# Reciprocals of a fused attention and gated-cell kernel: through DRAM instead of PE transposes

## Chip, cores and metric

One core of one Trainium2 chip. The metric is the device time of one execution of the program in microseconds; the median of several executions counts.

## The reference

`x` and `ctx` are (8, 512, 512) in float32. First a cross attention with a local window, then a gated recurrence over the batch axis:

```python
q = layernorm(x); k = v = ctx                      # 16 heads of 32
scores = einsum(q, k) / sqrt(32); scores[|i - j| > 64] = -inf
x = x + softmax(scores) @ v @ W_proj.T + b_proj
z = layernorm(x)
for t in range(8):                                 # c is (512, 512)
    f = sigmoid(z[t] @ wf.T + c @ uf.T + bf)
    i = sigmoid(z[t] @ wi.T + c @ ui.T + bi)
    g = tanh(z[t] @ wc.T + c @ uc.T + bc)
    c = f * c + i * g
out = x + tanh(z @ wo.T + c @ uo.T + bo)
```

## The kernel before

The attention works on 32 tiles of 128 query rows (4 for each of 8 batch entries). A tile has four slots, one for each group of 4 heads. The recurrence of batch entry b is 12 units (3 gates by 4 groups of 128 outputs); a unit is a sum of 8 cell products (4 for entry 0, whose state is the same for all rows), each with a high and a low part of both operands, so that one product is three PE matmuls (L499 to L501, 128x512).

One list, `steps`, sets the order of all engines: each engine walks it in order and takes its own part of each step, with semaphores between them. The list is written by the loop at L133: for slot n, i = n // 4 is the tile and s = n % 4 the slot in the tile. From slot 20 on (`early` is false) a slot holds, in this order:

- `turn` n: PE transposes the exponentials of the slot (L542), ACT copies them to `probs_t` (L682)
- for s = 1 `query` of tile i + 1 (PE, L510), for s = 2 `turn2` of tile i - 1 (PE L607, ACT L702, DVE L822), for s = 3 `spread` of tile i (PE L586, ACT L686)
- two cell products
- `score` n + 2: PE (L523), then DVE adds the mask and takes the row minimum (L767); `ln2b` for s = 1 (L816), `mult` for s = 3 (L796)
- `exp` n + 1: ACT (L677); `value` n: PE (L563, L568)
- gates and blends whose cell products are complete (ACT L719; DVE L851 to L868), states of the entry (ACT L731, DVE L879)
- `recip` n + 1: DVE (L774), POOL (L483); `sides` n + 1: three or six small DVE transposes of `probs` (L790)
- for s = 0: `ln1b` of tile i + 1 (DVE L758), `proj`, `resid` and `stat2` of tile i - 1 (PE products L499 to L501 into `ps_m`, DVE L801), loads; for s = 3 `halves` of tile i (ACT L690, POOL L478)
- the remaining cell products: one for entry 0 (slots 20 to 34), four afterwards.

The sums of the exponentials lie one query per partition, but the attention, `ps_v`, has queries along its free axis and the head's dimensions along the partitions. So `recip` takes the reciprocal of the sums (`invsum`), POOL copies each over 32 columns (`recip`), four PE transposes turn the tile's 128x512 block into `ps_m` (`spread`), ACT copies that to `tile_row`, and DVE multiplies `ps_v` with it (`mult`):

```python
if kind == "spread":
    pe.wait_ge(inv, G * (i + 1))
    ...
    for g in range(G):
        mm = pe.transpose(ps_m[:, g * P:(g + 1) * P], recip[:, g, :], ident[:, :])
```

`value` of a tile's first slot overwrites `ps_v` and waits for that multiplication (`attn_t`, L550). `halves` splits the result into `attn_hi` and `attn_lo`, for which `proj` waits (L597). SP issues all loads and stores of the steps in list order, one after the other.

## Time and profile before

| | us |
|---|---|
| median of 3 runs (1013.83 to 1017.21) | 1015.32 |
| profiled execution | 1014.71 |
| its span | 1012.7 |
| PE busy in the span | 981.4 (97%) |
| DVE, ACT, POOL busy | 609.7, 500.7, 226.1 |
| chain that ended last | PE 90%, DVE 4%, ACT 2% |

A row of a timeline gives the start in us from the span's start, the length in us, engine and line of the kernel, the operation with output and inputs, the count where like instructions were merged, and in brackets the idle time before it and who released it. Ends of PE matmuls are modelled and overlap the next start, so distances between starts tell what one costs. The span has three parts: tiles 0 to 4 without cell products, to about 105 us; tiles 5 to 31 with cell products, to about 839 us; the output products.

### The profile page before, as it was taken

The page shows a single profiled execution, that of the slowest core. Times are in us where ns is not written, and L with a number is a line of the kernel's source. Part 1 is how long each engine was busy: PE and PEld are TensorE (multiplying, and loading weights), DVE is VectorE, ACT ScalarE, POOL GpSimd, SP SyncE. Part 2 cuts the span into 40 slices and gives each one's busy share as a digit, 9 for nine tenths or more (in the row PEclk, how much of TensorE's full clock was granted, in tenths as well). Part 3 has the DMA queues.
Part 4 walks back from the last instruction along what each step waited for, and adds up shares of the span by engine and source line. Part 5 has one row for each costly group of instructions (what it writes and reads, how often), then busy time and mean ns, then how long its engine had stood idle before and what let it go on. Part 6 is the DMA issues. An engine that isn't in the chain of part 4 may idle for free.

```text
span 1012.7 us, 20229 instructions
## 1 busy us (share of the span) xinstructions
PE 981.4 (97%) x7028; PEld 739.8 (73%) x7028; DVE 609.7 (60%) x2211; ACT 500.7 (49%) x1473; POOL 226.1 (22%) x320
## 2 busy tenths in 40 slices
PE   6888999999999999999999999999999999999998
PEld 3454566777777777777777777777777778888886
DVE  5775887776567755866677656765577632133222
ACT  5776666555454554554465455554455432131222
POOL 4554322211111111211111112111111110002354
PEclk9998999999999999999999999999999999999999
DMA  8455322222222212212222222111112003029676
GB/s 270 122 164 166 110 74 80 84 80 73 79 85 79 66 61 75 63 54 74 79 85 79 74 79 84 58 53 47 43 35 72 12 20 126 1 81 376 226 231 208
DMA packets 76245, 99.36 MB, mean 98 GB/s; under 512 B 5233, under 2 KB 46193, under 8 KB 74609
## 3 DMA queue, kind: packets, MB, share of 16 engines
q1 hardware_dynamic: 75424, 97.80, 30.6%
q8 instruction: 57, 0.93, 0.4%
q10 hardware_dynamic: 720, 0.27, 0.2%
q14 instruction: 44, 0.35, 0.1%
HBM read 68.69 MB, written 29.36 MB: 97 GB/s over the span
## 4 chain that ended last, share of the span: by engine, by line
PE 90%; DVE 4%; ACT 2%; issue 2%; DMA 1%; POOL 0%; SPq 0%; DVEq 0%; ACTq 0%
PE ps_g L499 18%; PE ps_g L501 17%; PE ps_g L500 17%; PE ps_a L523 7%; PE ps_a L542 4%; PE ps_v L563 3%; PE ps_m L499 3%; PE ps_m L501 3%; PE ps_m L500 3%; PE ps_m L594 2%; PE ps_a L499 2%; PE ps_a L500 2%; PE ps_a L501 2%; PE ps_v L568 2%; ACT probs L677 1%
## 5 line engine op out<-in xcount | busy, mean ns | idle before, releaser
L767 DVE CUSTOM_DVE_ANT_0 probs<-ps_a,mask 128x192 f32<-128x192 f32 (+1 forms) x512 | 169.3, 387 | 162.8 <-PE ps_a L523 153.3
L677 ACT ACTIVATE probs<-probs,rowmin 128x192 f32<-128x192 f32 (+1 forms) x512 | 239.1, 473 | 1.7 <-DVE rowmin L767 1.7
L719 ACT ACTIVATE gate<-ps_g,bias 128x512 f32<-128x512 f32 x84 | 57.8, 688 | 211.2 <-PE ps_g L501 211.2
L790 DVE STREAM_TRANSPOSE probs_t<-probs 32x128 f32<-32x128 f32 x492 | 146.5, 298 | 6.0
L483 POOL COPY recip<-invsum 128x128 f32<-128x128 f32 x128 | 37.4, 292 | 493.4 <-DVE invsum L774 493.2
L499 PE MATMUL ps_g<-state_hi,gate_w 128*128 128x512 f32 x336 | 138.2, 411 | 0.0
L682 ACT ACTIVATE probs_t<-ps_a 128x512 f32<-128x512 f32 x108 | 64.3, 596 | 147.1 <-PE ps_a L542 146.5
L501 PE MATMUL ps_g<-state_hi,gate_w 128*128 128x512 f32 x336 | 131.4, 391 | 0.0
L500 PE MATMUL ps_g<-state_lo,gate_w 128*128 128x512 f32 x336 | 131.3, 391 | 0.0
L677 ACT ACTIVATION_READ_ACCUMULATOR probs<-probs,rowmin 128x1 f32 x512 | 98.5, 192 | 0.0
L523 PE MATMUL ps_a<-keys,queries 32*128 32x256 f32 (+1 forms) x1024 | 86.1, 406 | 2.2 <-DVE rowmin L767 1.4
L499 PE MATMUL ps_g<-x2t_even,gate_w 128*128 128x512 f32 x192 | 82.2, 428 | 0.0
L499 PE MATMUL ps_g<-x2t_odd,gate_w 128*128 128x512 f32 x192 | 79.2, 412 | 0.0
L501 PE MATMUL ps_g<-x2t_even,gate_w 128*128 128x512 f32 x192 | 75.5, 393 | 0.0
L501 PE MATMUL ps_g<-x2t_odd,gate_w 128*128 128x512 f32 x192 | 75.3, 392 | 0.0
L500 PE MATMUL ps_g<-x2t_even,gate_w 128*128 128x512 f32 x192 | 75.2, 392 | 0.0
L500 PE MATMUL ps_g<-x2t_odd,gate_w 128*128 128x512 f32 x192 | 75.1, 391 | 0.0
L499 PEld LDWEIGHTS ps_g<-state_hi,gate_w 128*128 128x128 f32 x336 | 63.1, 188 | 14.7 <-issue 2.4
L523 PEld LDWEIGHTS ps_a<-keys,queries 32*128 32x128 f32 x1024 | 40.8, 186 | 45.1 <-issue 42.1
L501 PEld LDWEIGHTS ps_g<-state_hi,gate_w 128*128 128x128 f32 x336 | 63.1, 188 | 13.7
L500 PEld LDWEIGHTS ps_g<-state_lo,gate_w 128*128 128x128 f32 x336 | 63.3, 188 | 10.7
L542 PE MATMUL ps_a<-ident,probs 128*128 128x128 f32 x432 | 65.6, 272 | 0.4 <-ACT probs L677 0.2
(182 smaller groups left out, 1754.4 us busy)
## 6 DMA issues: line engine op xcount, KB each, us to landing
values<-ctx_rows SPq DMA_DIRECT2D x34, 256.0 KB, 4.4
xr<-x SPq DMA_DIRECT2D x32, 256.0 KB, 3.8
keys<-ctx_t SPq DMA_DIRECT2D x16, 512.0 KB, 4.1
x_dram<-xr SPq DMA_DIRECT2D x32, 256.0 KB, 4.2
gate_w<-x2t_dram SPq DMA_DIRECT2D x8, 1024.0 KB, 10.6
keys<-ctx_t SPq DMA_DIRECT2D x16, 384.0 KB, 3.5
x2t_dram<-x2t_even SPq DMA_DIRECT2D x12, 512.0 KB, 3.8
x2t_dram<-x2t_odd SPq DMA_DIRECT2D x12, 512.0 KB, 3.8
```

The costliest lines, as they stand in the source:

```text
L483: pool.tensor_copy(recip[:, i % G, :].rearrange("p (h d) -> p h d", h=HPG), invsum[:, i // G % 2, i % G, :].unsqueeze(2).to_broadcast([P, ...
L499: pe.matmul(ps, lhs[0], rhs[0], start=start, stop=False)
L500: pe.matmul(ps, lhs[0], rhs[1], start=False, stop=False)
L501: return pe.matmul(ps, lhs[1], rhs[0], start=False, stop=stop)
L523: mm = pe.matmul(ps_a[h][:, 0:seen], queries[rows, g, :], keys[rows, tile % 2, g, 0:seen], start=True, stop=True)
L542: mm = pe.transpose(ps_turn[i][:, h * P:(h + 1) * P], probs[:, i % 2, h, own:own + P], ident[:, :])
L563: pe.matmul(ps_v[HEAD * h:HEAD * (h + 1), g * P:(g + 1) * P], values[:, tile % 2, 0, d], probs_t[:, h, :], start=True, stop=False)
L677: act.activation(row, row, ACT.Exp, bias=rowmin[:, i % 2, h:h + 1], scale=-1.0, accum_out=rowsum[:, i // G % 2, i % G, h:h + 1]).then_inc( ...
L682: act.activation(probs_t[:, 0:HPG, :], ps_turn[i][:, :].rearrange("p (a q) -> p a q", a=HPG), ACT.Copy)\
L719: act.activation(gate[:, min(gt, 1), :], ps_g[i % 2][:, :], ACT.Tanh, bias=(first_bias if b == 0 else bias)[:, gt, m:m + 1], scale=1.0 if ...
L767: dve.tensor_tensor_reduce(probs[:, i % 2, h, 0:SEEN[t]], ps_a[h][:, 0:SEEN[t]], mask[:, MASK0[t]:MASK0[t] + SEEN[t]], -SCALE, -NEG, ALU.a ...
L790: turn = dve.transpose(probs_t[BLK * keys_of:BLK * (keys_of + 1), HPG:2 * HPG, q], probs[q, i % 2, :, col:col + BLK])
```

## The change

From tile 5 on, the spread on PE and ACT and the broadcast on POOL are gone. Instead the reciprocals of a tile are kept in 32 columns of `invsum` (16 in use), DVE transposes these in 32x32 blocks to `invsum_t`, SP writes this to `recip_dram`, waits for its landing, and reads it back with each row of 128 queries repeated over 32 partitions (`send`, once after the third slot's reciprocal for three groups, once after the fourth's for the last). `mult` and `halves` of a tile move to the head of the next tile, behind `turn`; `mult` reads the reciprocals from `recip`. In s = 0, part of the remaining cell products goes ahead of `proj`: two from slot 36 on, none before. `proj` also waits for `x2_lo`, since `spread` no longer does so in front of it. The small statistics tiles are joined in one, `moments`.

```diff
...
@@ -140,20 +140,21 @@
             tile_steps("stat2", i - 1)
         if n < SLOTS:
             steps.append(("turn", n))
+        if s == 0 and i > WHOLE:
+            tile_steps("mult", i - 1)
+            tile_steps("halves", i - 1)
         if n - 1 in row_at:
             steps.append(("column", row_at[n - 1]))
         if early:
             steps.append(("exp", n + 1))
         else:
             if s > 0:
-                tile_steps((None, "query", "turn2", "spread")[s], (None, i + 1, i - 1, i)[s])
+                tile_steps((None, "query", "turn2", None)[s], (None, i + 1, i - 1, -1)[s])
             cells(2)
         if n + 2 < SLOTS:
             steps.append(("score", n + 2))
         if s == 1:
             tile_steps("ln2b", i - 1)
-        if s == 3 and not early:
-            tile_steps("mult", i)
         if early:
             tile_steps(("proj", "query", "turn2", "spread")[s], (i - 1, i + 1, i - 1, i)[s])
         elif n + 1 < SLOTS:
@@ -167,12 +168,15 @@
         gates()
         if n + 1 < SLOTS:
             steps.append(("recip", n + 1))
+            if n + 1 >= OWN_BANKS and (n + 1) % G >= G - 2:
+                steps.append(("send", 2 * ((n + 1) // G) + (n + 1) % G - (G - 2)))
             if n + 1 >= OWN_BANKS:
                 steps.append(("sides", n + 1))
         if s == 0:
             tile_steps("ln1b", i + 1)
             tile_steps("bias", i + 1)
             if not early:
+                cells(PER_SLOT[min((n - FIRST_CELL) // (TT * G), B - 1)] // 2 - 1)
                 tile_steps("proj", i - 1)
                 tile_steps("resid", i - 1)
                 tile_steps("stat2", i - 1)
@@ -183,8 +187,6 @@
             tile_steps("ln1", i + 2)
         if s == 3 and early:
             tile_steps("mult", i)
-        if s == 3 and i >= WHOLE:
-            tile_steps("halves", i)
         if FIRST_CELL <= n < FIRST_CELL + 2:
             steps.append(("split_proj", PAIR * (n - FIRST_CELL)))
         if n in split_slots:
@@ -193,7 +195,8 @@
             steps.append(("half_bias", 0))
             steps.append(("halve_c0", 0))
         if n >= FIRST_CELL:
-            cells(PER_SLOT[min((n - FIRST_CELL) // (TT * G), B - 1)] - 2)
+            more = PER_SLOT[min((n - FIRST_CELL) // (TT * G), B - 1)] - 2
+            cells(more - more // 2 if s == 0 else more)
         renew()
         n += 1
         if n == SLOTS + G:
@@ -250,6 +253,7 @@
 
         probs_t = sb("probs_t", [P, 2 * HPG, P], F32)
         recip = sb("recip", [P, G, P], F32)
+        recip_row = recip[:, :, :].rearrange("p g q -> p (g q)")
         attn_hi = sb("attn_hi", [P, G, P], F32R)
         attn_lo = sb("attn_lo", [P, G, P], F32R)
 
@@ -261,19 +265,22 @@
         bp_row = sb("bp_row", [P, D], F32)
         rowmin = sb("rowmin", [P, 2, HPG], F32)
         rowsum = sb("rowsum", [P, 2, G, HPG], F32)
-        invsum = sb("invsum", [P, 2, G, HPG], F32)
+        invsum = sb("invsum", [P, HEAD], F32)
+        inv_rows = invsum[:, 0:HPG * G].rearrange("p (h g) -> p h g", h=HPG)
+        invsum_t = sb("invsum_t", [P, HEAD], F32)
...
@@ -387,6 +395,19 @@
                 if kind == "ln2b":
                     sp.wait_ge(x1_done, i + 1)
                     sp.dma_start(x1_rows[i], xr[:, i % XR, :]).then_inc(x1_out[i % XR], DMA)
+                if kind == "send":
+                    tile, part = i // 2, i % 2
+                    sent = i - 2 * WHOLE
+                    sp.wait_ge(inv_turned, sent + 1)
+                    sp.dma_start(recip_dram[i].rearrange("c (a j) -> a c j", j=HEAD), invsum_t[:, :])\
+                      .then_inc(recip_sent, DMA)
+                    sp.wait_ge(recip_sent, DMA * (sent + 1))
+                    sp.wait_ge(spread, WHOLE)
+                    sp.wait_ge(attn_t, tile)
+                    first, last = (0, (G - 1) * P) if part == 0 else ((G - 1) * P, G * P)
+                    rows = recip_dram[i, 0:HPG * G, :].rearrange("(h g) q -> h (g q)", h=HPG)[:, first:last]
+                    sp.dma_start(recip_row[:, first:last],
+                                 rows.unsqueeze(1).to_broadcast([HPG, HEAD, last - first])).then_inc(recip_in, DMA)
                 if kind == "turn2" and b < B - 2:
                     sp.wait_ge(x2_lo, i + 1)
                     sp.dma_start(x2t_dram[b, :, :, :, t * P:(t + 1) * P],
@@ -477,11 +498,11 @@
                     need(pool, projected, i)
                     pool.tensor_tensor(attn_lo[:, :, :], attn, attn_hi[:, :, :].bitcast(F32), ALU.subtract)\
                         .then_inc(attn_split, 1)
-                if kind == "recip":
+                if kind == "recip" and i < OWN_BANKS:
                     pool.wait_ge(inverted, i + 1)
                     need(pool, spread, i // G)
                     pool.tensor_copy(recip[:, i % G, :].rearrange("p (h d) -> p h d", h=HPG),
-                                     invsum[:, i // G % 2, i % G, :].unsqueeze(2).to_broadcast([P, HPG, HEAD]))\
+                                     inv_rows[:, :, i % G].unsqueeze(2).to_broadcast([P, HPG, HEAD]))\
                         .then_inc(inv, 1)
                 if kind == "stat2":
                     pool.wait_ge(var2, i + 1)
@@ -586,6 +607,7 @@
                         mm = pe.transpose(ps_m[:, g * P:(g + 1) * P], recip[:, g, :], ident[:, :])
                     mm.then_inc(spread, 1)
                 if kind == "proj":
+                    need(pe, x2_lo, i)
                     if i == 0:
                         pe.wait_ge(wp_in, DMA)
                     if i < WHOLE:
@@ -736,6 +758,7 @@
 
         @block.vector
         def _(dve):
+            dve.memset(invsum[:, :], 0.0).then_inc(padded, 1)
             dve.wait_ge(consts, 6)
             for kind, i in steps:
                 if kind == "ln1":
@@ -770,8 +793,16 @@
                 if kind == "recip":
                     r, g = i // G % 2, i % G
                     dve.wait_ge(expd, HPG * (i + 1))
-                    need(dve, inv, i - 2 * G + 1)
-                    dve.reciprocal(invsum[:, r, g, :], rowsum[:, r, g, :]).then_inc(inverted, 1)
+                    if i == 0:
+                        dve.wait_ge(padded, 1)
+                    need(dve, inv, min(i - G + 1, OWN_BANKS))
+                    need(dve, inv_turned, 2 * (i // G - WHOLE) + (g == G - 1))
+                    dve.reciprocal(inv_rows[:, :, g], rowsum[:, r, g, :]).then_inc(inverted, 1)
+                if kind == "send":
+                    sent = i - 2 * WHOLE
+                    dve.wait_ge(inverted, G * (i // 2) + G - 1 + i % 2)
+                    need(dve, recip_sent, DMA * sent)
+                    dve.transpose(invsum_t[:, :], invsum[:, :]).then_inc(inv_turned, 1)
                 if kind == "turn" and i < OWN_BANKS:
                     some = min(SEEN[i // G % TT] - P, P)
                     dve.wait_ge(turned_2, i + 1)
@@ -791,9 +822,15 @@
                                              probs[q, i % 2, :, col:col + BLK])
                     turn.then_inc(turned_b, 1)
                 if kind == "mult":
-                    dve.wait_ge(recip_out, i + 1)
                     dve.wait_ge(valued, G * (i + 1))
-                    dve.tensor_tensor(tile_row[:, :], ps_v[:, :], tile_row[:, :], ALU.mult).then_inc(attn_t, 1)
+                    if i < WHOLE:
+                        dve.wait_ge(recip_out, i + 1)
+                        dve.tensor_tensor(tile_row[:, :], ps_v[:, :], tile_row[:, :], ALU.mult).then_inc(attn_t, 1)
+                    else:
+                        dve.wait_ge(recip_in, 2 * DMA * (i - WHOLE + 1))
+                        dve.wait_ge(q_turned, min(i + 2, TILES))
+                        dve.wait_ge(x2_turned, i)
+                        dve.tensor_tensor(tile_row[:, :], ps_v[:, :], recip_row, ALU.mult).then_inc(attn_t, 1)
                 if kind == "resid":
                     row = xr[:, i % XR, :]
                     dve.wait_ge(projected, i + 1)
...
```

PE from the end of the score product in the first slot of tile 17. Before:

```order
L523 MATMUL ps_a<-keys,queries 128x256 x3
L563 MATMUL ps_v<-probs_t,values 32x128 [waits v_in1,attn_t,turned_b,turned_a]
L563 MATMUL ps_v<-probs_t,values 32x128 x3
L568 MATMUL ps_v<-probs_t,values 32x128 x4
L499 MATMUL ps_m<-proj_w,attn_hi 128x512 [waits attn_split,wp_lo]
L500 MATMUL ps_m<-proj_w,attn_hi 128x512
L501 MATMUL ps_m<-proj_w,attn_lo 128x512
L499 MATMUL ps_m<-proj_w,attn_hi 128x512
L500 MATMUL ps_m<-proj_w,attn_hi 128x512
L501 MATMUL ps_m<-proj_w,attn_lo 128x512
```

After:

```order
L544 MATMUL ps_a<-keys,queries 128x256 x3
L584 MATMUL ps_v<-probs_t,values 32x128 [waits v_in1,attn_t,turned_b,turned_a]
L584 MATMUL ps_v<-probs_t,values 32x128 x3
L589 MATMUL ps_v<-probs_t,values 32x128 x4
L520 MATMUL ps_g<-x2t_odd,gate_w 128x512
L521 MATMUL ps_g<-x2t_odd,gate_w 128x512
L522 MATMUL ps_g<-x2t_odd,gate_w 128x512
L520 MATMUL ps_g<-x2t_odd,gate_w 128x512
L521 MATMUL ps_g<-x2t_odd,gate_w 128x512
L522 MATMUL ps_g<-x2t_odd,gate_w 128x512
L520 MATMUL ps_m<-proj_w,attn_hi 128x512 [waits attn_split,wp_lo,x2_lo]
L521 MATMUL ps_m<-proj_w,attn_hi 128x512
```

The three rows of a cell product stand twice between the value products (L563 and L568, now L584 and L589) and the projection, which was next to them before.

DVE from the last mask of the fourth slot of tile 16 to the first mask of the next slot. Before:

```order
L767 ISA probs,rowmin<-ps_a,mask 128x256
L767 ISA rowmin 128x1
L796 TENSOR_TENSOR tile_row<-ps_v,tile_row 128x512 [waits valued,recip_out]
L865 SCALAR_TENSOR_TENSOR gate<-gate,state 128x512 [waits gated]
L868 SCALAR_TENSOR_TENSOR state<-gate 128x512 [waits kept]
L774 RECIPROCAL invsum<-rowsum 128x4 [waits inv,expd]
L790 STREAM_TRANSPOSE probs_t<-probs 32x4x32 [waits valued,expd]
L790 STREAM_TRANSPOSE probs_t<-probs 32x4x32 x5
L767 ISA probs,rowmin<-ps_a,mask 128x256 [waits turned_b,expd,scored]
```

After:

```order
L790 ISA probs,rowmin<-ps_a,mask 128x256
L790 ISA rowmin 128x1
L902 SCALAR_TENSOR_TENSOR gate<-gate,state 128x512 [waits gated]
L905 SCALAR_TENSOR_TENSOR state<-gate 128x512 [waits kept]
L800 RECIPROCAL invsum<-rowsum 128x4 [waits inv_turned,inv,expd]
L821 STREAM_TRANSPOSE probs_t<-probs 32x4x32 [waits valued,expd]
L821 STREAM_TRANSPOSE probs_t<-probs 32x4x32 x5
L833 TENSOR_TENSOR tile_row<-ps_v,recip 128x512 [waits q_turned,x2_turned,recip_in,valued]
L790 ISA probs,rowmin<-ps_a,mask 128x256 [waits turned_b,expd,scored]
```

The multiplication stood ahead of blends, reciprocal and side blocks, and now stands behind them, ahead of the next masks.

SP from the store of `x1` in the second slot of a tile on. Before:

```order
L389 DMA x_dram<-xr 128x512 [waits x1_done]
L392 DMA x2t_dram<-x2t_odd 1024x1x128 [waits x2_lo]
L362 DMA xr<-x 128x512 [waits x2_done,x1_out3]
L365 DMA keys<-ctx_t 128x4x192 [waits scored]
```

After:

```order
L397 DMA x_dram<-xr 128x512 [waits x1_done]
L402 DMA recip_dram<-invsum_t 4x32x32 [waits inv_turned]
L409 DMA recip<-recip_dram 128x1x384 [waits attn_t,spread,recip_sent]
L413 DMA x2t_dram<-x2t_odd 1024x1x128 [waits x2_lo]
L402 DMA recip_dram<-invsum_t 4x32x32 [waits inv_turned]
L409 DMA recip<-recip_dram 128x1x128 [waits attn_t,spread,recip_sent]
L370 DMA xr<-x 128x512 [waits x2_done,x1_out3]
L373 DMA keys<-ctx_t 128x4x192 [waits scored]
```

Two pairs of a write and a read of `recip_dram` are new, one ahead of the store of `x2t` and one behind it, and with them a wait of SP for each write.

## Rows read from the trace of the kernel before

**Rows 1.** Busy us by stretch: length, PE, PEld, DVE, ACT, POOL; PEclk; DMA share, GB/s.
```profile
195.00:802.00 607.00, 607.00 (x4577) 463.76 (x4576) 405.35 (x1528) 318.16 (x967) 107.07 (x176) 1.00 0.22 66
```

**Rows 2.** PE: one tile's line, then the timeline (start us, us, engine, line).
```profile
L586 PE MATMUL ps_m<-ident,recip x128: 272/273/329, 24.1 to 822.6; 128*128 128x128 f32 x128
...
408.95 0.60 PE L542 MATMUL ps_a<-ident,probs 128*128 128x128 f32 x4
...
409.74 0.48 PE L499 MATMUL ps_g<-x2t_even,gate_w 128*128 128x512 f32 x1
...
415.26 0.60 PE L542 MATMUL ps_a<-ident,probs 128*128 128x128 f32 x4
415.62 0.48 PE L499 MATMUL ps_g<-x2t_odd,gate_w 128*128 128x512 f32 x1
```

**Rows 3.** Timeline of PE, turns with `recip` set in the early slots.
```profile
122.96 0.60 PE L542 MATMUL ps_a<-ident,probs 128*128 128x128 f32 x4
124.30 0.66 PE L586 MATMUL ps_m<-ident,recip 128*128 128x128 f32 x4 [0.73 <-POOL recip L483]
124.71 0.48 PE L499 MATMUL ps_g<-x2t_even,gate_w 128*128 128x512 f32 x1
...
187.34 0.60 PE L542 MATMUL ps_a<-ident,probs 128*128 128x128 f32 x4
...
189.19 0.48 PE L499 MATMUL ps_g<-x2t_even,gate_w 128*128 128x512 f32 x1
```

**Rows 4.** Timeline of DVE around the heads at 415.26 and 443.26.
```profile
413.45 0.69 DVE L796 TENSOR_TENSOR tile_row<-ps_v,tile_row 128x512 f32<-128x512 f32 x1
...
415.47 1.85 DVE L790 STREAM_TRANSPOSE probs_t<-probs 32x128 f32<-32x128 f32 x6
...
435.52 0.17 DVE L774 RECIPROCAL invsum<-rowsum 128x4 f32<-128x4 f32 x1
```

**Rows 5.** Timeline of PE from the head at 415.26.
```profile
417.83 0.43 PE L563 MATMUL ps_v<-probs_t,values 128*32 128x128 f32 x8
...
418.40 0.50 PE L499 MATMUL ps_m<-proj_w,attn_hi 128*128 128x512 f32 x1
...
424.42 0.60 PE L510 MATMUL ps_m<-ident,tile_row 128*128 128x128 f32 x4
...
443.26 0.60 PE L542 MATMUL ps_a<-ident,probs 128*128 128x128 f32 x4
```

**Rows 6.** Timelines of ACT and POOL around the same head.
```profile
414.17 0.63 ACT L690 ACTIVATE attn_hi<-tile_row 128x512 fp32r<-128x512 f32 x1
...
416.39 0.50 ACT L677 ACTIVATE probs<-probs,rowmin 128x256 f32<-128x256 f32 x1
...
415.87 1.30 POOL L478 TENSOR_TENSOR attn_lo<-tile_row,attn_hi 128x512 fp32r<-128x512 f32 x1
```

**Rows 7.** Timelines of PE and DVE around two early heads.
```profile
128.30 0.63 PE L542 MATMUL ps_a<-ident,probs 128*128 128x128 f32 x3
...
137.53 0.63 PE L510 MATMUL ps_m<-ident,tile_row 128*128 128x128 f32 x4 [0.61 <-DVE xr L801]
...
151.09 1.01 PE L542 MATMUL ps_a<-ident,probs 128*128 128x128 f32 x4
...
158.56 0.60 PE L510 MATMUL ps_m<-ident,tile_row 128*128 128x128 f32 x4
...
130.25 1.85 DVE L790 STREAM_TRANSPOSE probs_t<-probs 32x128 f32<-32x128 f32 x6
...
146.61 0.17 DVE L774 RECIPROCAL invsum<-rowsum 128x4 f32<-128x4 f32 x1
```

**Rows 8.** DMA issues (out<-in, queue, count, KB each, us from issue to landing).
```profile
values<-ctx_rows SPq DMA_DIRECT2D x44, 128.0 KB, 4.2
...
out<-xr SPq DMA_DIRECT2D x20, 256.0 KB, 2.1
...
values<-x_dram SPq DMA_DIRECT2D x8, 256.0 KB, 6.3
```

More of the change, by code:

```diff
@@ L21, in bass_xattn_ffn @@
 def bass_xattn_ffn(nc, x, ctx_rows, ctx_t, w_proj, b_proj, w_gates, u_gates, biases, w_out, u_out, b_out, in_c,
-                   out, x1_dram, x2t_dram):
+                   out, x1_dram, x2t_dram, recip_dram):
     B, T, D = x.shape
@@ L269, in bass_xattn_ffn @@
         st1 = sb("st1", [P, 2, 6], F32)
-        mv1 = sb("mv1", [P, 2, 2], F32)
-        ve1 = sb("ve1", [P, 2], F32)
-        rs1 = sb("rs1", [P, 2], F32)
         st2 = sb("st2", [P, 2, 6], F32)
-        mv2 = sb("mv2", [P, 2, 2], F32)
-        ve2 = sb("ve2", [P, 2], F32)
-        rs2 = sb("rs2", [P, 2], F32)
+        moments = sb("moments", [P, 4, 4], F32)
+        mv1, mv2 = [moments[:, a, :].rearrange("p (r m) -> p r m", r=2) for a in range(2)]
+        ve1, rs1 = moments[:, 2, 0:2], moments[:, 2, 2:4]
+        ve2, rs2 = moments[:, 3, 0:2], moments[:, 3, 2:4]
         ps_a = [pb(f"ps_a{h}") for h in range(HPG)]
@@ L290, in bass_xattn_ffn @@
         x2t_out = [sem("x2t_out0"), sem("x2t_out1")]
+        recip_sent = sem("recip_sent"); recip_in = sem("recip_in")
         raw_in = sem("raw_in"); bo_in = sem("bo_in")
@@ L300, in bass_xattn_ffn @@
         stat1 = sem("stat1"); aggr1 = sem("aggr1"); var1 = sem("var1"); ln1 = sem("ln1")
-        masked = sem("masked"); inverted = sem("inverted"); turned_b = sem("turned_b"); cleared = sem("cleared")
+        masked = sem("masked"); inverted = sem("inverted"); inv_turned = sem("inv_turned"); padded = sem("padded"); turned_b = sem("turned_b"); cleared = sem("cleared")
         attn_t = sem("attn_t"); x1_done = sem("x1_done")
@@ L932 @@
     B, T, D = arrays["x"].shape
+    recip_dram = nc.dram_tensor("recip_dram", (2 * B * T // P, HEAD, P), F32, kind="Internal").ap()
     x2t_dram = nc.dram_tensor("x2t_dram", (B, P, 2, D // P, T), F32, kind="Internal").ap()
@@ L935 @@
                    [d["w_c"], d["w_i"], d["w_f"]], [d["u_c"], d["u_i"], d["u_f"]],
-                   [d["b_c"], d["b_i"], d["b_f"]], d["w_out"], d["u_out"], d["b_out"], d["in_c"], out, x1_dram, x2t_dram)
+                   [d["b_c"], d["b_i"], d["b_f"]], d["w_out"], d["u_out"], d["b_out"], d["in_c"], out, x1_dram, x2t_dram,
+                   recip_dram)
     r = run_bass_kernel_spmd(nc, [arrays], core_ids=[0])
```

## Prediction

> **What bounds the kernel now.** I read the busy time by stretch first, then the idle time of PE in front of its instructions, then the timeline of each engine around one head of a tile, then the DMA issues. From 195 to 802 us PE is busy for 607.00 of 607.00 us at a granted clock of 1.00, while DVE has 405 and ACT 318 [rows 1]: in this stretch the span is the sum of PE's instructions, and an instruction taken from PE is a gain unless a new wait fills the hole. Before it, from 105.42 to 194.73, lie the sixteen slots of batch 0's cell (three cell products a slot), where other engines set part of the pace. I call them the early slots, those after them the steady ones.
>
> **What the change removes from PE.** The four transposes of `recip` per tile, from tile 5 on: 27 sets. Each lasts 273 ns by itself, but they overlap, so I take the distance between starts. With the set, the first transpose of the turn starts at 408.95 and the next cell product at 409.74: 0.79 us. Without it, 415.26 to 415.62: 0.36 us, elsewhere 0.35 [rows 2]. A steady set costs 0.44 us, and there are 23: **10.1 us**. In the early slots there are four sets, and there PE also waits for POOL's broadcast of the reciprocals (0.73 us at 124.30). The same distances are 1.75 us in the first (122.96 to 124.71) and 1.85 in the last (187.34 to 189.19) [rows 3], with 1.48 and 1.59 between them; less 0.35 each this is **5.3 us**. ACT's copy of `ps_m` to `tile_row` and POOL's 108 broadcasts go too; both engines have idle time, so I cost them at nothing. Moving two cell products ahead of the projection costs PE nothing by itself.
>
> **What it moves: the head of a tile.** The multiplication now stands at the head of the next tile, and PE needs it at that slot's value product. Take the head at 415.26, with the heaviest load on DVE (six side blocks, two blends). Before, DVE does the multiplication at 413.45 (0.69 us, its tail overlapped) and the side blocks from 415.47 to 417.32 [rows 4]. Without the multiplication in front, they end at about head + 1.4, the multiplication at + 2.1; the value product starts at + 2.57 (417.83) [rows 5]. So it is in time by 0.5 us. ACT's rounding (0.63) and POOL's subtraction (1.30) [rows 6] then end at + 2.7 and + 4.1; the projection, before at + 3.14 (418.40) [rows 5], is wanted two products (1.37 us) later, at + 4.5. Hidden by 0.4 us: no cost. What is late next is ACT's exponentials of that slot: they start after the rounding, at + 2.7 where they stood at + 1.1 (416.39) [rows 6], and end at + 4.7, still before DVE is through with its masks and asks for them. Only where a state is rounded behind them does DVE's chain (state, reciprocal, side blocks, next normalization, residual) pass the query's transposes, at + 9.15: by about 0.1 us at the first steady head and at five later ones. I charge **0.5 us**.
>
> In the early slots no cell product stands ahead of the projection, and every head has a state to round. At 128.30 the side blocks end at + 3.8 [rows 7]; after the change at + 3.2, the multiplication at + 3.9, the rounding at + 4.6, the subtraction at + 5.9. PE wanted the projection at + 4.5. The exponentials end at + 6.7, state at + 8.0, side blocks at + 10.0, normalization and residual at + 11.3, and the query's transposes wait for that: before they start at + 9.23 (137.53) [rows 7]. That is **2.1 us** given back. At 151.09 only three side blocks stand in front; the same walk puts the subtraction at + 4.7, the end of the projection at + 7.6, the query at + 8.9, against + 7.47 (158.56) before: **1.4 us**, and again 1.4 at the third head.
>
> **What it adds.** Two DVE transposes of 128x32 per tile (no row of this size; the side block is 0.31 us, nothing is the other end; 0.1 to 0.3 each, I take 0.1 because each partition has a quarter of the side block's elements). They stand in the second and third slots of a tile, where DVE idles: nothing. On SP's queue come four DMAs per tile, and SP waits in between for its own write to land; queued behind it are the store of `x2t`, the next `load_x` and `load_k`. Those buffers are used most of a tile (some 27 us) later: nothing. What matters is the chain from the last reciprocal to the multiplication: write of 16 KB, then broadcast read of 64 KB. The rows bound a transfer: 2.1 us for a store of 256 KB, 4.2 for loads of 128 KB [rows 8]. Between 4.2 and 8.4 us for the pair I take 2.1 for the write, since it is a store, and the middle, 3.2, for the read, plus 0.3 for transpose and hand-over: 5.6 us. In the steady slots the reciprocal ends at 435.7 and the next head is at 443.26, or 442.8 without the set; the multiplication may start at head + 1.9: 9.0 us are there [rows 4, 5]. Hidden, even at 8.4. In the early slots there are 6.3 us at the first head, 5.2 at the second (146.78 to 149.96 + 2.0) [rows 7] and about 5.1 at the third: late by 0.4 and 0.5, **0.9 us**.
>
> The Trainium skill, "DMA: Bandwidth & Descriptors" (the section on the two cost components), states a fixed 2.0 us and 436 GB/s. By it the pair would take an estimated 4.2 us and the 0.9 us would go. No row here shows so small a store.
>
> **Sum.** 10.1 + 5.3 - 0.5 - 2.1 - 1.4 - 1.4 - 0.9 = 9.1 us. The profiled execution took 1014.7 (span 1012.7), so 1005.6 like for like; against the median of 1015.3 it gives **1006.2 us**. Terms after the attention (PE's output products) just shift.
>
> **Rivals.**
> (a) *The early waits do not come back.* PE's 5.3 us there stay gone, because the delayed engines catch up during the projection. For: PE's wait for DVE's residual in front of the query was only 0.61 us [rows 7]. Against: in each head multiplication, rounding, exponentials and state lie in one chain. Time: 1015.3 - 15.4 = 1000.
> (b) *The early transfers are late by the upper bound.* With 8.4 + 0.3 us for the pair the three heads lose 2.4, 3.5 and 3.6 us in place of 0.9: 1015, no change.
> (c) *The wait only changes its name at every head.* The steady margins are 0.4 and 0.5 us. If the multiplication or POOL's part is 0.9 us longer than walked, each of 24 heads gives back what its set saved: 1015 to 1016. Against: rows 4 to 6 measure every part.
> (d) *Slower: the round trip through memory paces each tile.* The point is 9.0 us; from 9.4 on a head loses more than its 0.44. The loads with 6.3 us [rows 8] give 12.6 + 0.3 for the pair: 3.9 us at 24 heads, some 7.5 at three: about 1120 us. DVE would stand at the multiplication, behind it its masks, on PE the value product. Against: 6.3 us belongs to a burst of loads at the end; the middle moves 66 GB/s [rows 1].
> (e) *Each transpose is worth its full length.* 108 x 273 ns = 29.5 us: 986. Against: a set takes 0.44 us of PE's time, and PE overlaps [rows 2]. The Trainium skill, "TensorE: Matmul & The Clock Gate", Part 4 (PE-mode transpose), gives about 275 ns for a 128x128 transpose within a kernel, which the 273 ns agree with; by it alone an estimated 29.7 us would go.
> (f) The change does what it says as far as PE's list shows: 27 sets are gone from it.
>
> **Chances.** Forecast with its own spread (1003 to 1010) 0.55; (a) 0.20; (b) 0.11; (c) 0.06; (d) 0.05; (e) 0.03. The range runs from (a) to 1011: it leaves out (c), (d), (e) and half of (b). About 0.3% (3 us) is what a measurement here can tell from no change, so faster means below 1012.3: all of the forecast, (a), (e) and half of (b), 0.84. Same is the rest of (b) and most of (c), 0.10; slower 0.06.
>
> **What would show it.** Right: `recip` transposes on PE fall from 128 to 20; a turn takes 0.35 us to the next cell product in the fourth slot; PE stays at 607 of 607 in the steady stretch; idle time appears before the projection and the query at three early heads, 1 to 2 us each; the pair of transfers takes 5 to 6 us. Wrong: idle time at the value product of steady heads, released by DVE's multiplication or a DMA, (c) or (d); no idle time at early heads, (a); early heads waiting for a DMA by 2 us and more, (b).

## The result, and the profile after

| | before | after |
|---|---|---|
| median, us | 1014.58 (1013.38 to 1017.21) | 1025.3 (1022.47 to 1029.49) |
| profiled execution | 1014.71 | 1026.02 |
| its span | 1012.7 | 1024.2 |
| PE, DVE busy | 981.4, 609.7 | 979.4, 625.0 |
| ACT, POOL busy | 500.7, 226.1 | 487.2, 194.9 |

The ratio of the times is 1.0109, with a 95% interval of 1.009 to 1.0127: **slower by 1.1%**, where the forecast was 1006.2 with a range of 1000 to 1011.

Page of the changed kernel: span, engines, granted clock in 40 slices, chain that ended last.

```profile
span 1024.2 us, 20049 instructions
...
PE 979.4 (96%) x6920; PEld 734.9 (72%) x6920; DVE 625.0 (61%) x2266; ACT 487.2 (48%) x1446; POOL 194.9 (19%) x212
...
PEclk9999988889999999999999999999999999999999
...
PE 85%; DVE 5%; DMA 4%; issue 2%; ACT 2%; SPq 1%; POOL 1%; DVEq 0%; ACTq 0%
```

PE has 108 instructions fewer, yet its busy time fell by 2.0 us only, and the clock shows why one should look early: four slices of 25.6 us, from 128 to 230, are at 8 tenths. The same line of the kernel before:

```profile
PEclk9998999999999999999999999999999999999999
```

It has 9 there. DMA, 1% of the chain before, is 4%.

To see where the time goes I took the start of each slot's `turn` on PE and subtracted the same slot's start before, both counted from the turn of slot 20. A growing number is time lost, and each part of the kernel answers for its own growth. Each of these numbers comes from one profiled execution; times and ratios are of medians. Up to slot 38 (the early slots and the fourth head) the changed kernel loses **20.6 us** (229.05 - 103.98 = 125.07, before 209.88 - 105.42 = 104.46). From there to slot 127 it gains **7.15 us**. From a head's turn to the next slot's it loses 4.7, 6.8, 8.2 and 5.5 us at the four early heads; in the slots without the set it gains 0.8, 0.7, 1.2 and 1.0, and 0.8 once more in the slot behind the first head. All that is lost is lost at four places. The four sets are worth 3.8 us there; the 0.8 behind the first head is not theirs, since experiment 10 keeps the sets and shows it too.

The steady stretch, busy time as in [rows 1]; then PE's waits from 104 to 215 us (total, times, longest).

```profile
195.00:802.00 607.00, 603.20 (x4514) 456.34 (x4513) 421.23 (x1583) 309.80 (x955) 82.93 (x89) 0.99 0.27 80
```

```profile
PE ps_v L584 <- DVE tile_row L833: 12.6, 4, 4.5
...
PE ps_m L520 <- POOL attn_lo L499: 3.5, 3, 1.5
```

In the steady stretch PE is busy for 603.2 of 607 us, and part of the missing 3.8 is the fourth head at 208. In the early slots it waits four times for the multiplication, for 12.6 us. The third early head, on each engine. PE first:

```profile
178.13 1.12 PE L563 MATMUL ps_a<-ident,probs 128*128 128x128 f32 x4
...
185.68 0.66 PE L584 MATMUL ps_v<-probs_t,values 128*32 128x128 f32 x8 [4.50 <-DVE tile_row L833]
...
187.70 0.76 PE L520 MATMUL ps_m<-proj_w,attn_hi 128*128 128x512 f32 x1 [1.14 <-POOL attn_lo L499]
...
190.82 0.63 PE L521 MATMUL ps_m<-proj_w,attn_hi 128*128 128x512 f32 x1
191.25 0.63 PE L522 MATMUL ps_m<-proj_w,attn_lo 128*128 128x512 f32 x1
...
192.98 0.40 PE L521 MATMUL ps_g<-x2t_even,gate_w 128*128 128x512 f32 x1
193.21 0.39 PE L522 MATMUL ps_g<-x2t_even,gate_w 128*128 128x512 f32 x1
```

DVE and SP at the same place:

```profile
175.21 0.21 DVE L805 STREAM_TRANSPOSE invsum_t<-invsum 128x32 f32<-128x32 f32 x1
...
184.85 0.69 DVE L833 TENSOR_TENSOR tile_row<-ps_v,recip 128x512 f32<-128x512 f32 x1 [4.10 <-issue]
...
175.54 0.56 SPq L413 DMA_DIRECT2D x2t_dram<-x2t_odd  x1
176.14 0.56 SPq L402 DMA_DIRECT2D recip_dram<-invsum_t  x1
181.65 0.53 SPq L409 DMA_DIRECT2D recip<-recip_dram  x1
```

The transpose of the reciprocals begins at 175.21 and the multiplication at 184.85: 9.6 us, where the prediction had 5.6. SP issues the write at 176.14, 0.60 us behind the store of `x2t`, and the read 5.51 us later, once the write has landed; the multiplication starts 3.20 us after that. DVE has stood there for 4.10 us ("issue": the profile shows no releaser; the one semaphore left open is the read's), PE for 4.50. At the other heads DVE waits 0.2, 2.2 and 2.3 us, and the second write takes 4.85, 5.72 and 5.25 us from issue to the read's issue. The same pair of instructions late in the kernel, when SP has no store of `x2t` to issue:

```profile
806.84 0.53 SPq L402 DMA_DIRECT2D recip_dram<-invsum_t  x1
808.79 0.53 SPq L409 DMA_DIRECT2D recip<-recip_dram  x1
```

Here the write takes 1.95 us, near the 2.1 of the prediction. What differs is what stands ahead of it on the queue. At the third head that is the read for the first three groups (192 KB, issued at 174.96) and the store (512 KB). The trace's list of DMA packets shows the order: the write's 128 packets of 128 bytes run from 180.6 to 181.2, and of the store's 1024 packets of 512 bytes 1006 start before the first of them. At 806.84 the first packet comes 1.2 us after the issue.

Then comes what the prediction did not have at all. Products in the projection start every 0.43 us (190.82 to 191.25), and from 192.98 on every 0.23. Stretches of the same head, columns as in [rows 1]:

```profile
183.00:185.00 2.00, 0.00 (x0) 0.00 (x0) 0.15 (x1) 0.00 (x0) 0.00 (x0) 1.00 0.53 164
185.00:187.00 2.00, 0.87 (x16) 0.66 (x16) 1.64 (x9) 1.43 (x6) 0.72 (x1) 0.67 0.00 0
187.00:189.00 2.00, 1.30 (x3) 1.14 (x4) 0.50 (x1) 1.47 (x6) 0.55 (x1) 0.50 0.00 0
189.00:191.00 2.00, 2.00 (x6) 1.52 (x6) 1.75 (x6) 0.00 (x0) 0.08 (x1) 0.50 0.00 0
191.00:193.00 2.00, 2.00 (x8) 1.54 (x7) 0.05 (x1) 0.00 (x0) 1.19 (x1) 0.63 0.00 0
193.00:195.00 2.00, 2.00 (x14) 1.75 (x13) 1.67 (x4) 1.36 (x3) 0.15 (x1) 1.00 0.00 0
```

PE idles for 4.5 us, the granted clock falls from 1.00 to 0.50 (2.4 to 1.2 GHz), and nearly the whole projection runs at that. A busy PE at half clock looks like a busy PE: only the clock column tells it apart. There are four such stretches of 6.8 us, one at each early head; the kernel before has none between 105 and 1010 us (each kernel has one at its end, which no clock remark below counts). So there are three suspects: the chain of moved work, the round trip through memory, the clock.

### The profile page after: what moved, and what is told of

Same layout as the page of the kernel before. It is cut to its first block, busy times and chain, and to the rows that moved or that the text cites. A ratio compares the mean times of both kernels' runs of the same rounds, so it can differ in the third digit from the quotient of the medians.

```text
span 1024.2 us, 20049 instructions
## 1 busy us (share of the span) xinstructions
PE 979.4 (96%) x6920; PEld 734.9 (72%) x6920; DVE 625.0 (61%) x2266; ACT 487.2 (48%) x1446; POOL 194.9 (19%) x212
## 4 chain that ended last, share of the span: by engine, by line
PE 85%; DVE 5%; DMA 4%; issue 2%; ACT 2%; SPq 1%; POOL 1%; DVEq 0%; ACTq 0%
PE ps_g L520 17%; PE ps_g L522 16%; PE ps_g L521 16%; PE ps_a L544 6%; PE ps_a L563 4%; PE ps_v L584 3%; PE ps_m L520 3%; PE ps_m L521 3%; PE ps_m L522 3%; DMA recip_dram<-invsum_t 3%; PE ps_m L616 2%; PE ps_a L520 2%; PE ps_a L522 2%; PE ps_a L521 2%; PE ps_v L589 2%
## 5 line engine op out<-in xcount | busy, mean ns | idle before, releaser
L478 POOL TENSOR_TENSOR moments<-moments,half 128x1 f32<-128x1 f32 x32 | 19.4, 607 | 315.2 <-DVE moments L772 315.2
L499 POOL TENSOR_TENSOR attn_lo<-tile_row,attn_hi 128x512 fp32r<-128x512 f32 x27 | 34.6, 1283 | 192.9 <-ACT attn_hi L712 192.9
```

The source lines that it names most:

```text
L499: pool.tensor_tensor(attn_lo[:, :, :], attn, attn_hi[:, :, :].bitcast(F32), ALU.subtract)\
```

## The experiments

"Growth" is the number above: time lost against before up to slot 38, then what slots 38 to 127 add. After has +20.6 and -7.15.

**1. No wait for the transfers.** The multiplication reads the projection's bias row in place of the reciprocals, so it leaves them out; the transfers still run.

```diff
-                        dve.wait_ge(recip_in, 2 * DMA * (i - WHOLE + 1))
+                        dve.wait_ge(bp_in, DMA)
...
-                        dve.tensor_tensor(tile_row[:, :], ps_v[:, :], recip_row, ALU.mult).then_inc(attn_t, 1)
+                        dve.tensor_tensor(tile_row[:, :], ps_v[:, :], bp_row[:, :], ALU.mult).then_inc(attn_t, 1)
```

> Left out: the multiplication reads the projection's bias row in place of the reciprocals, so it does not wait for the two transfers; the transfers still run, everything else is as in the changed kernel. Theory A (at the early heads the round trip through memory is late, PE stands at the value product for 2.3 to 4.5 us, and its clock then runs at half for 6.8 us): PE's waits on DVE's multiplication fall from 12.9 us to under 1, no stretch at half clock after the first 105 us, and 1005 to 1007 us. Theory B (the work moved to the head, multiplication, rounding, subtraction, is too long a chain there, transfers or not): each early head still loses 5 to 8 us, 1020 us or more.

Measured: 1013.31 us, ratio 0.9993 (0.9979 to 1.0008); growth +5.1, -7.1; granted clock 0.50 in two stretches of 3.4 us instead of four of 6.8. So the wait for the transfers, with what it sets off, costs 12 us, more than the 10.7 by which the change is slower. But the kernel doesn't reach the forecast either: the early slots lose 5.1 instead of nothing. First early head, PE and DVE:

```profile
125.57 0.66 PE L565 MATMUL ps_a<-ident,probs 128*128 128x128 f32 x4
...
130.40 0.43 PE L586 MATMUL ps_v<-probs_t,values 128*32 128x128 f32 x8 [2.14 <-DVE tile_row L835]
...
125.08 0.42 DVE L792 CUSTOM_DVE_ANT_0 probs<-ps_a,mask 128x256 f32<-128x256 f32 x1
...
127.68 1.85 DVE L823 STREAM_TRANSPOSE probs_t<-probs 32x128 f32<-32x128 f32 x6
129.56 0.69 DVE L835 TENSOR_TENSOR tile_row<-ps_v,bp_row 128x512 f32<-128x512 f32 x1
```

The multiplication starts at head + 4.0, the prediction had + 3.2 (it ends there at + 3.9). DVE's masks of the fourth slot still run at the head (125.08): I had hung them on PE's scores, which come sooner without the set, but DVE itself, busy with the third slot's work, sets them. PE waits 2.14 us for the multiplication.

**2. Only the move, reciprocals still turned on PE.**

```diff
+    FROM = 32
+    HEADS = 5
...
-        if s == 0 and i > WHOLE:
+        if s == 0 and i > HEADS:
...
-                tile_steps((None, "query", "turn2", None)[s], (None, i + 1, i - 1, -1)[s])
+                tile_steps((None, "query", "turn2", "spread")[s], (None, i + 1, i - 1, i if i < FROM else -1)[s])
```

> Multiplication and halves at the head of the next tile as in the changed kernel, but the reciprocals spread by PE, ACT and POOL as before; no transfers. Theory A: the steady slots take what they took before, the early heads give back 1 to 2 us each because the projection waits for POOL's subtraction, clock full after 105 us: 1017 to 1020 us. Theory B: the early heads lose as much as in the changed kernel, with stretches at half clock: 1033 us or more.

Measured: 1020.8 us, 1.0066 (1.0047 to 1.0085); growth +6.3, +0.6. With no transfer and no set removed, the move alone costs 6.3 us in the early slots. Against the expectation the clock did not stay full: it is 0.50 for 3.4 us from 180.1 on, in the third head's projection, after PE had waited 1.47 us for the subtraction. That head loses 3.1 us, the two before it 1.6 and 1.4. Up to 1.7 of the 6.3 are thus the clock's, and the rest, 4.5, agrees with the 4.9 of the prediction's walk. Its waits of PE from 104 to 215 us begin with the first line; the second is the stretch behind the clock's fall, columns as in [rows 1]:

```profile
PE ps_m L526 <- POOL attn_lo L505: 4.3, 3, 1.5
```

```profile
180.00:184.00 4.00, 4.00 (x12) 3.12 (x11) 2.24 (x6) 0.49 (x1) 1.36 (x2) 0.57 0.02 4
```

The wait is the projection behind the later subtraction, as walked. Experiment 1 has the same move without the sets, and its early growth is smaller by 1.1 us only. That is what taking the early sets away brings once the move is there, or 2.8 if the half-clock stretches (two there, one here) are taken out at half their length, where the prediction had 5.3. In the steady slots the move is nearly free, and the difference to after's -7.15, 7.75 us, is what taking the sets away adds there.

**3. PE kept busy while it waits**: products that nobody reads, before the first value product of the four heads.

```diff
+                        for r in range({6: 8, 7: 12, 8: 18, 9: 10}.get(tile, 0)):
...
+                            pe.matmul(ps_m[:, :], proj_w[:, 0, 0, 0:P], proj_w[:, 0, 1, :], start=True, stop=True)
```

> The changed kernel with 8, 12, 18 and 10 matmuls of 128x512 without use (into ps_m, which is free there) in front of PE's wait for the multiplication at the four early heads, so that PE is busy where it stood idle. If the idle time is what lowers the clock: no stretch at half clock after 105 us, and about 4 x 3.4 = 13.7 us less than the changed kernel, 1011 to 1014 us. If the clock falls for another reason: half-clock stretches as before, 1025 us or a little more.

Measured: 1019.42 us, 1.0051 (1.0033 to 1.007); growth +11.2, -7.1; no stretch at half clock, but less gained than the 11 to 14 us expected. The window from 125 to 215 us of after and of this kernel (before, PE is busy for 86.04 of these 90 us at 1.00):

```profile
125.00:215.00 90.00, 72.94 (x562) 52.20 (x552) 60.52 (x236) 45.02 (x141) 12.21 (x14) 0.87 0.28 82
```

```profile
125.00:215.00 90.00, 83.62 (x651) 59.99 (x650) 65.46 (x251) 48.21 (x149) 13.05 (x15) 1.00 0.29 87
```

**48 additional products make the kernel faster**: 5.9 us by the medians, 9.4 by the growth. The clock is a term of its own. What is left, still 5 us slower than before, is waiting with the clock full.

**4. The store of `x2t` behind the reciprocals** in SP's queue.

```diff
-                if kind == "turn2" and b < B - 2:
...
+                if kind == "turn2" and i < WHOLE - 1:
+                    store_x2t(i)
+                if kind == "send" and i % 2 == 1:
+                    store_x2t(i // 2 - 1)
```

> The changed kernel with the 512 KB store of x2t issued behind the tile's last write and read of the reciprocals instead of in front of them. If the second write is slow because it goes behind that store: it lands in some 2.8 us instead of 4.9 to 5.7, the multiplication's waits for the transfer at the second to fourth early head (2.2, 4.1 and 2.3 us) fall to under 1.5 together, and the time comes near that of the kernel without the wait, 1012 to 1016 us. If a write of 128 B rows takes 5 us by itself: 1025 us as before.

Measured: 1015.92 us, 1.0012 (0.9999 to 1.0025); growth +7.9, -7.1; three half-clock stretches of 3.4 us. SP and DVE at the third head:

```profile
171.19 0.53 SPq L409 DMA_DIRECT2D recip_dram<-invsum_t  x1
174.76 0.53 SPq L416 DMA_DIRECT2D recip<-recip_dram  x1
175.34 0.56 SPq L369 DMA_DIRECT2D x2t_dram<-x2t_odd  x1
...
177.60 0.69 DVE L840 TENSOR_TENSOR tile_row<-ps_v,recip 128x512 f32<-128x512 f32 x1 [1.11 <-issue]
```

The write to the read's issue takes 3.57 us (3.82, 2.75 and 3.95 at the others) instead of 5.51. One move in a queue gives back 9.4 us of the change's loss. The write, 16 KB, had waited behind the store's 512 KB in the same queue; here it still stands behind the read of 192 KB, and in later tiles, where that read is done by then, it takes as little as 1.95 us here too. The store itself lands after 5.4 to 5.9 us at the early heads of the kernel after, where it follows that read by 0.6 us, and after 3.8 to 4.2 here. The Trainium skill, "DMA: Bandwidth & Descriptors" (Two DMAs through the same engine are not ordered), says that descriptors of one queue of a DMA engine start in order; the trace agrees, by the order of the packets and by 5.5 us behind the store against 3.6 ahead of it. The Trainium skill's fixed 2.0 us, from the same page (the section on the two cost components) and fitted there to DMAs issued from POOL, was weighed by the prediction. The writes from SP that have nothing ahead of them agree with it, 1.95 us from issue to the read's issue; it holds no wait in the queue.

**5. `send` on POOL's queue.**

```diff
-                if kind == "send":
...
+                    pool.dma_start(recip_dram[i].rearrange("c (a j) -> a c j", j=HEAD), invsum_t[:, :])\
```

> The changed kernel with the four transfers of a tile issued from POOL's queue instead of SP's. If the order within SP's queue is what delays them: as the expectation for the store moved back, 1012 to 1016 us. If the load on the shared DMA engines delays them: 1022 us or more. If issuing from POOL is slower by itself (POOL stands in the wait for the write, with the subtraction behind it), steady heads lose too and it ends above 1026 us.

Measured: 1064.33 us, 1.0481 (1.0438 to 1.0524); growth +26.7, +20.6: the third case of the expectation. Two of its waits:

```profile
PE ps_v L584 <- DVE tile_row L833: 45.5, 21, 6.9
...
POOL recip L494 <- DMA recip_dram<-invsum_t: 147.6, 54, 4.8
```

Here rival (d) is seen, at the place it names: PE's value product waits for the multiplication in 21 slots, for 45.5 us. POOL stands 147.6 us for the writes, with its own subtraction behind them. So the experiment doesn't tell order in a queue from load on the engines, as it was meant to; the packets above do. The Trainium skill, "DMA: Bandwidth & Descriptors" (Issuing engines are not separate DMA queues), says another issuing engine saves only the time to issue; nothing was saved here.

**6. The change from tile 9 on only**, with move and transfers, the early slots as before.

```diff
+    FROM = 9
+    HEADS = 9
...
-            if n + 1 >= OWN_BANKS and (n + 1) % G >= G - 2:
+            if n + 1 >= G * FROM and (n + 1) % G >= G - 2:
```

> Tiles 5 to 8 as in the kernel before (spread on PE, multiplication in the fourth slot), from tile 9 on through memory as in the changed kernel. Theory A and B alike: the early slots take what they took before (89.3 us from turn 20 to turn 36), the steady slots gain as in the changed kernel, 23 x 0.43 less some 1 us at heads: 1005 to 1006 us. If a loss of the changed kernel lies outside the early slots, it stays above 1008.

Measured: 1006.36 us, 0.9922 (0.9903 to 0.9941); growth 0.0, -7.35. The early slots' loss is gone whole, and the steady gain stays. What keeps it from 22 x 0.44 = 9.7 are five heads where a state is rounded and six side blocks are due. From the head to the query's transposes in tile 13, PE, here:

```profile
302.38 0.60 PE L569 MATMUL ps_a<-ident,probs 128*128 128x128 f32 x4
...
311.27 0.60 PE L569 MATMUL ps_a<-ident,probs 128*128 128x128 f32 x4
311.98 0.63 PE L537 MATMUL ps_m<-ident,tile_row 128*128 128x128 f32 x4
```

and DVE:

```profile
308.10 0.69 DVE L922 SCALAR_TENSOR_TENSOR state_lo<-state,state_hi 128x512 fp32r<-128x512 f32 x1 [1.56 <-ACT state_hi L759]
...
311.15 0.68 DVE L844 TENSOR_TENSOR xr<-ps_m,xr 128x512 f32<-128x512 f32 x1
```

The transposes start 0.71 us after the turn, where 0.43 is the rule (before, 313.71 to 314.15). DVE waited for ACT's rounding of the state, which stands behind the halves and the exponentials.

**7. As 6, exponentials ahead of the halves, three cell products ahead of the projection.**

```diff
-            tile_steps("halves", i - 1)
...
+        if s == 0 and i > HEADS:
+            tile_steps("halves", i - 1)
...
+                ahead = 3 if i > HEADS else ahead
```

> As mixed (memory from tile 9 on), and at the head ACT does the next slot's exponentials ahead of rounding the attention, with three instead of two cell products in front of the projection. In the changed kernel five steady heads, those with a state to round and six side blocks, each lose 0.48 us. If that comes from the exponentials standing behind the late multiplication (state, reciprocal, side blocks, residual, query late): 1.5 to 2.4 us less than mixed, 1004 to 1005 us. If only from the value product waiting for the multiplication (0.27 us each): under 1 us to be seen at those heads elsewhere, and 1006 us stays.

Measured: **1005.34 us**, 0.9904 (0.9888 to 0.9921), the fastest of all; growth 0.0, -8.55. PE at the same head, 9.29 us from head to transposes where 6 has 9.60 and before had 9.15:

```profile
302.96 0.60 PE L572 MATMUL ps_a<-ident,probs 128*128 128x128 f32 x4
...
311.81 0.60 PE L572 MATMUL ps_a<-ident,probs 128*128 128x128 f32 x4
312.25 0.60 PE L540 MATMUL ps_m<-ident,tile_row 128*128 128x128 f32 x4
```

The traces differ by 1.2 us in the steady part; the two ratios' intervals overlap.

**8. As 6 from tile 8 on, with the late store of 4; and 9. the same with the order of 7.** The lines that differ from 6:

```diff
-    FROM = 9
-    HEADS = 9
+    FROM = 8
+    HEADS = 8
```

> Memory from tile 8 on, with the store of x2t behind the transfers. Tile 8's spread costs PE 1.5 us in the kernel before (its wait for POOL included). If the transfer is in time at its head once the store is out of the way: 1.0 to 1.2 us less than mixed, about 1005.3 us. If it is late there: a wait of 1 to 2 us and a stretch at half clock, 1007 to 1009 us.

> Memory from tile 8 on, the store of x2t behind the transfers, and the exponentials ahead of the rounding at the head. mixed_order gained 1.2 us over mixed in the steady slots, from8_late 0.3 us in the early ones; both together: 1004.5 to 1005.0 us. If the rounding, now later, holds up the projection at tile 9's head: no better than mixed_order's 1005.3.

Measured: 1007.05 us, 0.9922 (0.9902 to 0.9941), growth to slot 38 -0.3; and 1007.2 us, 0.9923 (0.9897 to 0.9949), growth -0.1. Both miss their forecasts (1005.3; 1004.5 to 1005.0). Once the write stands ahead of the store, the fourth early head pays for itself, and no more.

**10 to 12. An idle PE without any transfer.** Kernel 6, plus six statistics passes that nobody reads ahead of `mult` of tiles 5 to 8 (10), and with 16 idle products on PE in two places (11: before the value product; 12: before the scores that wait).

```diff
+                if kind == "mult" and WHOLE <= i < 9:
+                    for r in range(6):
...
+                        dve.bn_stats(invsum_t[:, 0:6], bp_row[:, :]).then_inc(idle, 1)
```

and in 12, on PE:

```diff
+                    if g == 2 and WHOLE < tile <= 9:
...
+                        for r in range(16):
+                            pe.matmul(ps_m[:, :], proj_w[:, 0, 0, 0:P], proj_w[:, 0, 1, :], start=True, stop=True)
```

> mixed with six statistics instructions of 0.7 us without use on DVE in front of the multiplication of tiles 5 to 8 (some 4.5 us each), so that PE stands idle at four early heads without any transfer being involved. If idle time lowers the clock: stretches of 3.4 to 6.8 us at half clock behind these heads, each costing 1.7 to 3.4 us beside the 4 x 4.2 us of waiting: 1027 to 1034 us. If the clock fell in the changed kernel because of the transfers: no such stretch, 1022 to 1024 us.

> paused with 16 matmuls of 128x512 without use (3.7 us) on PE in front of the value product of those four heads, where it stood idle. The waiting of the other engines is the same. If idle time lowers the clock: no stretch at half clock there, and 7 to 13 us less than paused. If not: the same time as paused.

> paused again, with the 16 matmuls without use now in front of the score product of the four heads, where PE stood idle for 3.6 us each (in paused_filled they stood behind that wait and only came on top of it). DVE is late as in paused. If PE's idle time is what lowers the clock: no stretch at half clock from 125 us on, and 7 to 13 us less than paused, 1019 to 1025 us. If the lateness of the other engines does it, with PE busy or not: the same stretches and about 1032 us.

Measured: 10: 1032.04 us, 1.0171 (1.0156 to 1.0187), growth +23.7. 11: 1043.1 us, 1.0284 (1.0257 to 1.031), +34.0. 12: 1024.1 us, 1.009 (1.007 to 1.0109), +16.9. PE in 10 and its waits from 125 to 215 us:

```profile
135.62 1.24 PE L550 MATMUL ps_a<-keys,queries 32*128 32x256 f32 x8 [3.98 <-ACT probs_t L710]
...
PE ps_a L550 <- ACT probs_t L710: 11.6, 3, 4.0
```

Busy time and clock of 10, then of 12:

```profile
125.00:215.00 90.00, 75.28 (x568) 53.75 (x569) 71.00 (x239) 46.45 (x143) 14.91 (x26) 0.89 0.24 71
```

```profile
125.00:215.00 90.00, 84.12 (x657) 61.19 (x657) 76.25 (x253) 49.93 (x153) 16.42 (x26) 1.00 0.22 68
```

In 10 the granted clock is 0.50 in three stretches of 6.8 us and one of 3.4, the last behind 215 us. But its idle time stood somewhere I had not meant, in front of the scores, and 11 put its products behind it: they could cover nothing, the clock fell all the same (0.50 four times for 3.4 us), and their time came on top. 11 is a misplaced experiment, not evidence against the clock. 12 has the products where PE idles: clock 1.00, and 7.9 us less than 10. No transfer is on the path at these four heads, and DVE is as late in 12 as in 10, so it is PE's idle time that lowers the clock.

## Why the prediction was wrong, by its steps

**What the sets are worth: right in the steady slots, too high in the early ones.** `recip` transposes on PE fell from 128 to 20, and a steady tile gains 0.42 to 0.44 us where nothing else is late (term: 0.44). The early sets, charged 5.3, gave 3.8 in their slots (4.2 in experiment 1), and experiments 1 and 2 put their worth with the move in place at 1.1 to 2.8: PE came sooner to the heads and waited there for DVE and POOL. The step at fault is "less 0.35 each this is 5.3 us", which takes the whole wait for POOL's broadcast as saved. Rival (e), the full 273 ns each, is out: the steady part gained 7 to 8.6 us in every kernel with the sets gone and SP's queue.

**State at the head, charged 0.5: too small.** "By about 0.1 us at the first steady head and at five later ones": five heads lost 0.47 us each (in experiment 6, 302.38 to the turn at 318.00; before, 305.00 to 320.15), 2.4 in all. With them 22 x 0.44 = 9.7 becomes the 7.3 seen. The order of 7 brings most of it back. The mechanism was the one named, its size was off.

**The chain at the early heads, 4.9 us given back: about 6.4.** With the sets in place it was right (4.5, experiment 2). In experiment 1 the heads lose 9.3 us, of which up to 3.4 are the clock's (6.8 us at half of it): 5.9 at least. What failed is "after the change at + 3.2, the multiplication at + 3.9": it took DVE's masks as PE's to set, and they were DVE's own.

**The transfers at the early heads, 0.9 us: 8.6.** This is the step that made no change into a slower kernel: without it (experiment 1) the time is that of the kernel before, which is still 7 us short of the forecast. "I take 2.1 for the write, since it is a store" fits a write with nothing ahead of it (1.95); "queued behind it" is what failed: I asked what waits behind the new DMAs on SP's queue and never what stands ahead of them, at the third head 192 and 512 KB. Write 5.5, read and hand-over 3.2, and 0.9 from the transpose to the write's issue make 9.6 us, above even the upper bound of 8.4 + 0.3, which counted transfers but no queue. Rival (b) named late transfers and their sign in the profile (DVE waits 2.2, 4.1, 2.3), at a chance of 0.11, and its price for them, 9.5 us, was near the 8.6; it named no queue, and the clock was missing from it too.

**The clock: put at nothing without a reason.** All terms and rivals took PE's granted clock as 1.00, which [rows 1] shows of the steady slots, and the window of before from 125 to 215 us of the early ones, both with PE nearly always busy. Each early term made PE idle in 105 to 195 us, and what idle time does to the clock was asked nowhere, though the page of before had a slice at 8 in the first 105 us. It costs 9.4 us by experiment 3's growth, 5.9 by its median. The Trainium skill, "TensorE: Matmul & The Clock Gate" (Part 1), says that the throttled state is the default and activity releases it; experiments 10 and 12 agree, 3.98 us of idle and then 0.50, against 1.00 when PE is kept busy. By that rule, had I applied it, every head where the sum makes PE wait would have had a second price.

**Together.** 3.8 saved, then 6.4 of chain, 8.6 of late transfers and 9.4 of clock: +20.6 in the early part (an account by what each experiment took away; the chain's share is what is left, and it lies above experiment 1's lower bound of 5.9). With the steady -7.15 that is +13.5 at slot 127, of which the medians show 10.7. Of the remaining 2.8 us, 1.4 lie in the first 105 us of the two profiled executions (slot 20 starts at 103.98 and 105.42; the kernel before has 6.8 us at half clock there, the changed one 3.4) and 0.5 behind slot 127; the rest is between these executions and the medians.

**Rival (d)**, slower because the round trip paces each tile, had the sign, at a chance of 0.05, but not the place: the steady margin of 9.0 us held, with one wait of 0.3 us on PE after 215 us. Only POOL's queue (5) broke it.

## What to carry to other kernels

Take a saving where the engine is the bound and leave the old form where others pace it: the same edit gains 0.8% from tile 9 on and loses 1.1% from tile 5 on. Before putting a small DMA on a path that someone waits for, list what stands ahead of it in its queue, in bytes, and price a round trip through memory at its nearest measured row plus that. And whenever an edit makes PE idle by microseconds, read the granted clock of the stretch behind it, and price the work there at half speed. And a wait taken from one engine is saved only if the engine that it waits for next is early enough.

## What the runs showed of the hardware

- After 4.5 us of an idle PE the granted clock was 0.50 for 6.8 us, in which PE was idle for 1.1 and busy otherwise; 2.14 us of idle and 1.37 more shortly behind it brought 3.4 us of it (experiment 1). The length of the idle time alone doesn't tell: in experiment 2 a wait of 1.47 us was followed by 3.4 us at 0.50, and one of 1.45 at the head before was not. Products that nobody reads, in the idle time, kept it at 1.00 and made the kernel faster, twice (5.9 and 7.9 us).
- A write of 16 KB from 128 partitions took 1.95 us from its issue to the next instruction that waited for it with nothing ahead of it, 2.75 to 3.95 at early heads behind a read of 192 KB, and 4.85 to 5.72 behind that read and a store of 512 KB in the same queue; the broadcast read took 2.6 to 3.2 us to the multiplication.
- Four PE transposes of 128x128 in a row, 273 ns each, add 0.42 to 0.44 us to a busy PE's time.
